# Two selective scans on one core: states written to the product ring in SBUF and multiplied there in place, PSUM left with the decays alone

## The chip, the cores and the metric

The kernel runs on one core of a Trainium2 chip, as one launch. The metric is the device time in microseconds (us) of that core; the time before is 5297.91 us, the median of three runs.

## What is computed

A residual network of four layers on an input of 32 x 256 tokens with 128 features. Each layer is `x = x + s * silu(f)`, where `s` comes from a recurrent or attention block and `f` from a feed-forward block. The change touches only the selective scan, which is the recurrent block of layer 3 and a part of that of layer 2 (layers are counted from 0). Cut to what matters:

```python
# layer 2, for each token t, 256 channels, 16 states per channel
dA = exp(dt[..., None] * A)
h  = h * dA + dt[..., None] * B[:, None, :] * x[..., None]
y  = sum(h * C[:, None, :], -1)
# layer 3
A_bar = exp(dt[..., None] * A)
B_bar = (A_bar - 1.0) / safe_A * B[:, None, :]
h = A_bar * h + B_bar * x[..., None]
y = einsum('bds,bs->bd', h, C) + D * x
```

The state starts at zero at the first token of each of the 32 sequences.

## The kernel before

`mamba` (L1411) is called twice, with `l3` false for layer 2 and true for layer 3. Both work on 16 tiles of 512 tokens (2 sequences of 256). A tile has 16 **units** (256 per layer): one half `h` of the 256 channels, which fills the 128 partitions, and two of the 16 states, so a unit's arrays are 128 x 1024 values of float32. The engines run their own loops over the units `q` and are tied by semaphores alone; the order on each engine is the order in which the code is written. For a unit:

- ACT, `decay(q)` (L1642): two exponentials write the decays into the PSUM array `ps_h` (in the trace `mb_h`), which has two buffers. Decay q overwrites what unit q-2 left there, so it waits for the reader of that: the scan, when POOL multiplies the unit, or else DVE's product.
- POOL, `u` (L1743): `u = B * (dt x)` into a ring of four (`m_u`), from the broadcast rows `m_bsb` that SP fetches by DMA. The input of unit q waits until scan q-4 is done.
- DVE, `make(q)`: in layer 3 a `scalar_tensor_tensor` (L1772) turns `u` into `(decay - 1) * u`; in both layers a memset (L1775) then puts zeros at the 4 places of `ps_h` where a sequence begins, so that one scan can run over both sequences and both states.
- DVE, `scan(q)` (L1786): `tensor_tensor_scan`, from the decays in PSUM and `u` in SBUF. It writes into `ps_h` in place, or, for the units that POOL multiplies (`by_pool`: every fourth in layer 2, every second in layer 3), into one of two SBUF buffers `m_hs`.
- the product with C, `times_c(q)`: on DVE (L1795) from `ps_h` in PSUM and the rows `m_csb` in SBUF, on POOL (L1722) from `m_hs` and `m_csb`. Both write the ring `hc` of four units in SBUF (`m_hc`; in layer 3 it lies in the large array that the trace calls `r`).
- PE, `sum_states(q)` (L1506): matmuls that add the unit's two products into `ps_y`. They run strictly in the order of q.

DVE's loop is, for each q:

```python
scan(q)
if q + 1 < NU:
    make(q + 1)
if not by_pool[q]:
    times_c(q)
```

and POOL's is `u(q)`, then `times_c(q - 3)` if that unit is its own. Once per tile come other steps: on POOL `step_sizes` (two sums into `m_dt`, L1707, and in layer 2 the product `m_dtx`, L1713) and in layer 3 `gate_old` (L1727, L1730); on DVE `gated` (L1804), `finish` (L1811, L1813) and in layer 3 `fix` (L1766).

Another stage is read for one fact only: `attention_inputs`, in which DVE (L1913, L1924, L1931) and POOL (L1968, L1973) work beside each other on 128 x 512 arrays.

Of the kernel before, what the change touches and what calls it, by code (L numbers as in the profile page):

```python
# [7 lines left out]
ALU = mybir.AluOpType  # L8
ACT = mybir.ActivationFunctionType
# [1401 lines left out]
def mamba(nc, w, parts, l3, hp, res, out, bc_d, gate_of=None):  # L1411

    wconv, a_neg, diag_y, diag_d, conv_bias, corr = parts
    with ExitStack() as ctx:
        def sb(name, shape, dt=F32):
            return ctx.enter_context(nc.sbuf_tensor(("m3_" if l3 else "m2_") + name, shape, dt))
# [12 lines left out]
        bsb = sb("bsb", [P, RING, SG, TILE])  # L1429
        csb = sb("csb", [P, RING, SG, TILE])  # L1430
        u = sb("u", [P, RING, SG, TILE])
        hc = out[:, 6 * TILE:(6 + RING * SG) * TILE].rearrange("p (n s t) -> p n s t", n=RING, s=SG) if l3 \
            else sb("hc", [P, RING, SG, TILE])
        hs = sb("hs", [P, 2, SG, TILE])
        yg = sb("yg", [P, 2, TILE])
        warm = sb("warm", [P, 3 * NT + 2])
        names = " ".join(f"b_in{s}" for s in range(RING)) + " " + " ".join(f"c_in{s}" for s in range(RING))
# [24 lines left out]
        @block.tensor  # L1462
        def _(pe):

            def conv(a, h):
                if a:
                    pe.wait_ge(sg_ready, 2 * a)
                for k in range(TAPS):
                    mm = nc.tensor.matmul(ps_w[:, h], wconv[:, k, h * P:(h + 1) * P], padded_tile(hp, k)(a),  # L1469
                                          start=k == 0, stop=k == TAPS - 1)  # L1470
                mm.then_inc(xs_in, 1)

            def gate(a, h):
                pe.wait_ge(dt_taken, 2 * a + 1 + h)
                if h == out_bank and a >= 2:
                    pe.wait_ge(x_done, a - 1)
                nc.tensor.matmul(ps_w[:, h], w["in_w"][:, DI + h * P:DI + (h + 1) * P], padded_tile(hp)(a),
                                 start=True, stop=True).then_inc(gate_in, 1)

            def project_bc(a):  # L1480
                pe.wait_ge(xs_ready, 2 * a + 2)
                for h in range(2):
                    mm = nc.tensor.matmul(ps_w[:, 0], w["xp_bc"][:, h * P:(h + 1) * P], xs[:, a % 2, h], start=h == 0, stop=h == 1)
                mm.then_inc(bc_in, 1)

            def project_low(a):
                for h in range(2):
                    mm = nc.tensor.matmul(ps_w[0:64, 1], w["xp_low"][:, h * 64:(h + 1) * 64], xs[:, a % 2, h],
                                          start=h == 0, stop=h == 1)
                mm.then_inc(low_in, 1)  # L1490

            def step_size(a, h):
                K = 64 if l3 else NSTATE
                pe.wait_ge(low_ready, a + 1)
                nc.tensor.matmul(ps_w[:, h], w["dt_w"][0:K, h * P:(h + 1) * P], low[0:K],
                                 start=True, stop=True).then_inc(dt_in, 1)

            def sum_states(q):
                i, g, h = place(q)
                if by_pool[q]:  # L1500
                    pe.wait_ge(hp_ready, pool_units[q + 1])
                else:
                    pe.wait_ge(hc_ready, dve_units[q + 1])
                for s in range(SG):
                    weight = diag_y[:, h * NSTATE + g * SG + s] if l3 else w["eye"]
                    mm = nc.tensor.matmul(ps_y[:, h], weight, hc[:, q % RING, s], start=False, stop=g == GROUPS - 1 and s == SG - 1)  # L1506
                mm.then_inc(y_used, 1)

            def project_out(i):
                pe.wait_ge(yg_ready, 2 * i + 2)  # L1510
                pe.wait_ge(dt_taken, 2 * min(i + 2, NT))
                if i == NT - 1:
                    pe.wait_ge(sg_ready, 2 * NT)
                    pe.wait_ge(x_done, i)
                for h in range(2):
                    mm = nc.tensor.matmul(ps_w[:, out_bank], w["out_w"][:, h * P:(h + 1) * P], yg[:, h],
                                          start=h == 0, stop=h == 1)
                mm.then_inc(out_ready, 1)

            def project(a):  # L1520
                project_bc(a)
                if l3:
                    project_low(a)

            conv(0, 0)
            conv(0, 1)
            project(0)
            step_size(0, 0)
            step_size(0, 1)
            gate(0, 0)  # L1530
            gate(0, 1)
            for i in range(NT):
                more = i + 1 < NT
                if more:
                    conv(i + 1, 0)
                    conv(i + 1, 1)
                if i:
                    pe.wait_ge(yg_ready, 2 * i)
                for h in range(2):
                    nc.tensor.matmul(ps_y[:, h], diag_d[:, h], xs[:, i % 2, h], start=True, stop=False)  # L1540
                for n in range(UNITS):
                    sum_states(i * UNITS + n)
                    if n == (3 if l3 else 2) and more:
                        project(i + 1)
                    if n == (5 if l3 else 3) and more:
                        step_size(i + 1, 0)
                        step_size(i + 1, 1)
                    if n == (9 if l3 else 7) and i:
                        project_out(i - 1)
                    if n == (11 if l3 else 10) and more:  # L1550
                        gate(i + 1, 0)
                        gate(i + 1, 1)
            project_out(NT - 1)

        @block.scalar
        def _(act):
# [75 lines left out]
            def decay(q):  # L1632

                i, g, h = place(q)
                act.wait_ge(dt_ready, 2 * i + h + 1)
                if q >= 2 and by_pool[q - 2]:
                    act.wait_ge(h_ready, q - 1)
                if q >= 2 and not by_pool[q - 2]:
                    act.wait_ge(hc_ready, dve_units[q - 1])
                for s in range(SG):  # L1640
                    n = h * NSTATE + g * SG + s
                    ins = nc.scalar.activation(ps_h[:, q % 2, s], dt[:, i % 2, h], ACT.Exp, scale=a_neg[:, n:n + 1])  # L1642
                ins.then_inc(da_ready, 1)

            for n in range(UNITS):
# [54 lines left out]
        def _(pool):  # L1700
# [13 lines left out]
                    pool.wait_ge(dtx_ready, a + 1)  # L1714

            def times_c(q):
                n, k = q // 2, pool_units[q]
                pool.wait_ge(h_ready, q + 1)
                pool.wait_ge(c_in[n % RING], (n // RING + 1) * 16)
                if q >= RING:  # L1720
                    pool.wait_ge(y_used, q - RING + 1)
                nc.gpsimd.tensor_tensor(hc[:, q % RING], hs[:, k % 2], csb[:, n % RING], ALU.mult).then_inc(hp_ready, 1)  # L1722

            def gate_old(a):
                pool.wait_ge(x_done, a + 1)
# [30 lines left out]
        def _(dve):  # L1756
            V = nc.vector

            def flat(ap):
                return ap.rearrange("p s t -> p (s t)")  # L1760
# [6 lines left out]

            def make(q):
                dve.wait_ge(da_ready, q + 1)
                if l3:  # L1770
                    dve.wait_ge(u_ready, q + 1)  # L1771
                    V.scalar_tensor_tensor(out=flat(u[:, q % RING]), in0=flat(ps_h[:, q % 2]), scalar=-1.0,  # L1772
                                           in1=flat(u[:, q % RING]), op0=ALU.add, op1=ALU.mult).then_inc(made, 1)
                    dve.wait_ge(made, q + 1)
                V.memset(ps_h[:, q % 2].rearrange("p s (r t) -> p (s r) t", t=T)[:, :, 0:1], 0.0).then_inc(cleared, 1)  # L1775

            def scan(q):
                if not l3:
                    dve.wait_ge(u_ready, q + 1)
                dve.wait_ge(cleared, q + 1)  # L1780
                to = ps_h[:, q % 2]
                if by_pool[q]:
                    to = hs[:, pool_units[q] % 2]
                    if pool_units[q] >= 2:
                        dve.wait_ge(hp_ready, pool_units[q] - 1)
                V.tensor_tensor_scan(flat(to), flat(ps_h[:, q % 2]), flat(u[:, q % RING]), 0.0,  # L1786
                                     ALU.mult, ALU.add).then_inc(h_ready, 1)

            def times_c(q):
                n = q // 2  # L1790
                dve.wait_ge(h_ready, q + 1)
                dve.wait_ge(c_in[n % RING], (n // RING + 1) * 16)
                if q >= RING:
                    dve.wait_ge(y_used, q - RING + 1)  # L1794
                V.tensor_tensor(hc[:, q % RING], ps_h[:, q % 2], csb[:, n % RING], ALU.mult).then_inc(hc_ready, 1)  # L1795

            def gated(i):

# [16 lines left out]
            if l3:  # L1815
                fix(0, 0)
                fix(0, 1)
            make(0)
            for q in range(NU):
                i, n = q // UNITS, q % UNITS  # L1820
                scan(q)
                if q + 1 < NU:
                    make(q + 1)
                if not by_pool[q]:
                    times_c(q)
# [1571 lines left out]
```

## Time and profile before

| | us |
|---|---|
| median of three runs (5293.03 to 5308.22) | 5297.91 |
| the profiled execution, its own time | 5317.53 |
| its span | 5315.9 |
| scan stage of layer 2, window 2065 to 2950 | 885 |
| scan stage of layer 3, window 4210 to 5310 | 1100 |

Times in the trace are counted from the start of the span. A row of grouped instructions gives their number, their busy time, the mean of one in ns, and the time that the engine sat idle before them with what ended it. In a timeline a start can lie a few hundredths of a microsecond before the end of the instruction ahead, since the engines overlap the end of one with the beginning of the next.

### The profile page before, as it was taken

Reading aid. Unit: us, or ns where it says so; the run is one execution under the profiler, and the core shown is the slowest. Engines: PE = TensorE matmul, PEld = TensorE weight load, DVE = VectorE, ACT = ScalarE, POOL = GpSimd, SP = SyncE. Lnnn points to the kernel's source line nnn. Section 1 sums busy time; section 2 is a strip of 40 time slices with the busy share of each in tenths; the row PEclk is TensorE's granted clock in tenths of the full one; section 3 lists DMA queues with packets and bytes.
Section 4 is the critical chain, followed back from the end, with each engine's and each line's share of the span. In section 5 each row is a group of like instructions: output and inputs, shape, how many; then the busy total and the mean of one; then the engine's idle time right before and its main releaser. Section 6 shows DMA issues by size and latency. Waiting matters only on the chain. (4 is left out here: it accounts for less than half of the span.)

```text
span 5315.9 us, 46819 instructions
## 1 busy us (share of the span) xinstructions
PE 3899.6 (73%) x13216; PEld 1770.4 (33%) x13216; DVE 3623.8 (68%) x5296; ACT 2530.9 (48%) x3893; POOL 2938.8 (55%) x2250
## 2 busy tenths in 40 slices
PE   5444425895583997888887879998698877777776
PEld 2111202472231564333333345454243322222222
DVE  6999615312253775999999744444444499999999
ACT  4444311232152776666665334445236555555554
POOL 3887470105404445999999311112431288988987
PEclk7777756897786998999999988889798899999999
DMA  1110210121121113444444232331110243444442
GB/s 47 40 42 8 82 47 5 46 67 47 44 92 42 52 50 114 154 156 156 152 155 152 65 65 40 41 41 31 40 52 9 83 135 137 134 139 135 136 140 99
DMA packets 161696, 434.74 MB, mean 82 GB/s; under 512 B 28150, under 2 KB 51384, under 8 KB 160048
## 3 DMA queue, kind: packets, MB, share of 16 engines
q1 hardware_dynamic: 142512, 374.41, 23.0%
q0 software_dynamic: 18944, 57.57, 3.0%
q8 instruction: 97, 1.59, 0.1%
q14 instruction: 143, 1.17, 0.1%
HBM read 363.67 MB, written 68.68 MB: 81 GB/s over the span
## 5 line engine op out<-in xcount | busy, mean ns | idle before, releaser
L1642 ACT ACTIVATE mb_h<-m_dt,m_a_neg 128x512 f32<-128x512 f32 x1024 | 665.7, 682 | 720.3 <-DVE r L1795 330.6
L1506 PE MATMUL mb_y<-r,m_diag_y 128*128 128x512 f32 x1024 | 547.2, 669 | 271.1 <-POOL r L1722 158.8
L1786 DVE TENSOR_TENSOR_SCAN mb_h<-mb_h,m_u 128x1024 f32<-128x1024 f32 x320 | 733.9, 2293 | 10.4
L1743 POOL TENSOR_TENSOR m_u<-m_bsb,m_dtx 128x1024 f32<-128x1024 f32 x256 | 596.2, 2357 | 20.8 <-DVE mb_h L1786 13.6
L1506 PE MATMUL mb_y<-m_hc,w_common 128*128 128x512 f32 x1024 | 494.2, 622 | 147.7 <-DVE m_hc L1795 84.7
L1743 POOL TENSOR_TENSOR m_u<-m_bsb,m_xs 128x1024 f32<-128x1024 f32 x256 | 599.6, 2367 | 0.0
L1786 DVE TENSOR_TENSOR_SCAN m_hs<-mb_h,m_u 128x1024 f32<-128x1024 f32 x192 | 437.6, 2279 | 0.2 <-POOL m_u L1743 0.2
L2259 DVE TENSOR_REDUCE at_mx<-at_ps_s 128x4 f32<-128x512 f32 (+1 forms) x256 | 243.2, 958 | 235.4 <-PE at_ps_s L2073 235.2
L1506 PEld LDWEIGHTS mb_y<-r,m_diag_y 128*128 128x128 f32 x1024 | 195.7, 207 | 617.1 <-POOL r L1722 238.7
L1722 POOL TENSOR_TENSOR r<-m_hs,m_csb 128x1024 f32<-128x1024 f32 x128 | 304.9, 2382 | 120.4 <-DVE m_hs L1786 119.3
L1506 PEld LDWEIGHTS mb_y<-m_hc,w_common 128*128 128x128 f32 x1024 | 190.0, 195 | 443.9 <-issue 192.2
L1772 DVE SCALAR_TENSOR_TENSOR m_u<-mb_h,m_u 128x1024 f32<-128x1024 f32 x256 | 308.0, 1203 | 19.2 <-ACT mb_h L1642 19.2
L2191 ACT ACTIVATE at_pt<-at_ps_c 128x512 f32<-128x512 f32 x384 | 229.1, 607 | 173.1 <-PE at_ps_c L2101 122.1
L2217 POOL CAST at_nm<-at_mx 128x16 bf16<-128x16 f32 x64 | 12.7, 198 | 521.1 <-DVE at_mx L2259 521.1
L343 PE MATMUL d_ring<-r,w_l 128*128 128x512 f32 x128 | 91.6, 859 | 224.1 <-ACT d_fm L393 222.2
L1469 PE MATMUL mb_w<-r,m_wconv 128*128 128x512 f32 x512 | 234.4, 611 | 22.3 <-ACT m_sg L1570 11.5
L1795 DVE TENSOR_TENSOR m_hc<-mb_h,m_csb 128x1024 f32<-128x1024 f32 x192 | 235.1, 1225 | 3.5
L493 POOL TENSOR_TENSOR d_sq_q<-d_state,d_tm 128x512 f32<-128x512 f32 x128 | 161.9, 1270 | 91.2 <-DVE d_state L597 91.0
L2098 PE MATMUL at_ps_c<-at_q,at_k 75*128 75x512 bf16 x384 | 157.7, 411 | 46.5 <-ACT at_pt L2191 26.9
L1707 POOL TENSOR_TENSOR m_dt<-m_lin,m_sp 128x512 f32<-128x512 f32 x64 | 80.0, 1274 | 202.2 <-ACT m_sp L1598 202.2
L2073 PE MATMUL at_ps_s<-at_k,at_q 72*128 72x256 bf16 (+1 forms) x1024 | 176.3, 267 | 0.0
L1004 POOL DMA_INDIRECT x_slots<-r,l_slots x128 | 124.8, 975 | 86.1 <-DVEq L1047 44.6
(503 smaller groups left out, 8714.4 us busy)
## 6 DMA issues: line engine op xcount, KB each, us to landing
m_bsb<-bc_rows SPq DMA_DIRECT2D x256, 512.0 KB, 4.8
m_csb<-bc_rows SPq DMA_DIRECT2D x256, 512.0 KB, 3.9
at_q<-q_parts SPq DMA_DIRECT2D x144, 128.0 KB
x_slots<-d_zeros SPq DMA_DIRECT2D x8, 1024.0 KB, 5.1
kept_x<-r SPq DMA_DIRECT2D x2, 4096.0 KB
xg_xg<-x_slots SPq DMA_DIRECT2D x32, 256.0 KB
y_slots<-xg_yo POOLq DMA_DIRECT2D x32, 256.0 KB
xl_xg<-x_slots SPq DMA_DIRECT2D x32, 256.0 KB
```

What stands on the lines that cost most here:

```text
L493: G.tensor_tensor(sq_q[:, 2 * p:2 * p + 2], state[:, n % 3], qt.unsqueeze(2).broadcast_to([P, 2 * HL, D0, D0]), ALU.mult).then_inc(sq_read ...
L1469: mm = nc.tensor.matmul(ps_w[:, h], wconv[:, k, h * P:(h + 1) * P], padded_tile(hp, k)(a), start=k == 0, stop=k == TAPS - 1)
L1506: mm = nc.tensor.matmul(ps_y[:, h], weight, hc[:, q % RING, s], start=False, stop=g == GROUPS - 1 and s == SG - 1)
L1642: ins = nc.scalar.activation(ps_h[:, q % 2, s], dt[:, i % 2, h], ACT.Exp, scale=a_neg[:, n:n + 1])
L1722: nc.gpsimd.tensor_tensor(hc[:, q % RING], hs[:, k % 2], csb[:, n % RING], ALU.mult).then_inc(hp_ready, 1)
L1743: nc.gpsimd.tensor_tensor(u[:, q % RING], bsb[:, n % RING], dtx[:, i % 2, h].unsqueeze(1).broadcast_to([P, SG, TILE]), ALU.mult).then_inc( ...
L1772: V.scalar_tensor_tensor(out=flat(u[:, q % RING]), in0=flat(ps_h[:, q % 2]), scalar=-1.0, in1=flat(u[:, q % RING]), op0=ALU.add, op1=ALU.m ...
L1786: V.tensor_tensor_scan(flat(to), flat(ps_h[:, q % 2]), flat(u[:, q % RING]), 0.0, ALU.mult, ALU.add).then_inc(h_ready, 1)
L1795: V.tensor_tensor(hc[:, q % RING], ps_h[:, q % 2], csb[:, n % RING], ALU.mult).then_inc(hc_ready, 1)
L2073: mm = nc.tensor.matmul(ps_s[:, g % 2, d, 0:keys], q9[0:PARTS, slot, g * QPK + d, col:col + P], k9[0:PARTS, slot, g, row:row + keys], star ...
L2191: nc.scalar.activation(pt[:, u % 8], ps_c[:, u % 2], ACT.Exp).then_inc(exp_ready, 1)
L2259: V.tensor_reduce(mx[:, n % 2, g * QPK:(g + 1) * QPK], ps_s[:, g % 2, :, 0:(n % 2 + 1) * P], AX, ALU.max, negate=True).then_inc(max_ready, 1)
```

## The change

- Every scan now writes to the ring `hc` in SBUF, none to PSUM, and `hs` is gone. The ring has six units in layer 2 and five in layer 3 (`held`), and it is the scan, no longer the product, that waits until PE has summed the unit whose place it takes.
- The product with C is made in place in the ring, by DVE or POOL as before.
- PSUM holds decays alone. A decay waits only for the scan two units back, never for a product. In layer 2 the zeros are written once, at the start, and ACT leaves their columns out (`rows(to)[:, :, 1:T]`); `make` is gone from the loop there. In layer 3 `make` stays as it was.
- `project_out(i)` waits for the step sizes of tile i+2 instead of i+1.

```diff
-        hc = out[:, 6 * TILE:(6 + RING * SG) * TILE].rearrange("p (n s t) -> p n s t", n=RING, s=SG) if l3 \
-            else sb("hc", [P, RING, SG, TILE])
-        hs = sb("hs", [P, 2, SG, TILE])
+        held = 5 if l3 else 6
+        hc = out[:, 6 * TILE:(6 + held * SG) * TILE].rearrange("p (n s t) -> p n s t", n=held, s=SG) if l3 \
+            else sb("hc", [P, held, SG, TILE])
...
-                pe.wait_ge(dt_taken, 2 * min(i + 2, NT))
+                pe.wait_ge(dt_taken, 2 * min(i + 3, NT))
...
-                if q >= 2 and by_pool[q - 2]:
+                if q >= 2:
                     act.wait_ge(h_ready, q - 1)
-                if q >= 2 and not by_pool[q - 2]:
-                    act.wait_ge(hc_ready, dve_units[q - 1])
+                elif not l3:
+                    act.wait_ge(cleared, 1)
...
-                    ins = nc.scalar.activation(ps_h[:, q % 2, s], dt[:, i % 2, h], ACT.Exp, scale=a_neg[:, n:n + 1])
+                    to, step = ps_h[:, q % 2, s], dt[:, i % 2, h]
+                    if not l3:
+                        to, step = rows(to)[:, :, 1:T], rows(step)[:, :, 1:T]
+                    ins = nc.scalar.activation(to, step, ACT.Exp, scale=a_neg[:, n:n + 1])
...
-                if q >= RING:
-                    pool.wait_ge(y_used, q - RING + 1)
-                nc.gpsimd.tensor_tensor(hc[:, q % RING], hs[:, k % 2], csb[:, n % RING], ALU.mult).then_inc(hp_ready, 1)
+                nc.gpsimd.tensor_tensor(hc[:, q % held], hc[:, q % held], csb[:, n % RING], ALU.mult).then_inc(hp_ready, 1)
...
             def scan(q):
-                if not l3:
-                    dve.wait_ge(u_ready, q + 1)
-                dve.wait_ge(cleared, q + 1)
-                to = ps_h[:, q % 2]
-                if by_pool[q]:
-                    to = hs[:, pool_units[q] % 2]
-                    if pool_units[q] >= 2:
-                        dve.wait_ge(hp_ready, pool_units[q] - 1)
-                V.tensor_tensor_scan(flat(to), flat(ps_h[:, q % 2]), flat(u[:, q % RING]), 0.0,
+                if l3:
+                    dve.wait_ge(cleared, q + 1)
+                else:
+                    dve.wait_ge(da_ready, q + 1)
+                    dve.wait_ge(u_ready, q + 1)
+                if q >= held:
+                    dve.wait_ge(y_used, q - held + 1)
+                V.tensor_tensor_scan(flat(hc[:, q % held]), flat(ps_h[:, q % 2]), flat(u[:, q % RING]), 0.0,
                                      ALU.mult, ALU.add).then_inc(h_ready, 1)
 
             def times_c(q):
                 n = q // 2
                 dve.wait_ge(h_ready, q + 1)
                 dve.wait_ge(c_in[n % RING], (n // RING + 1) * 16)
-                if q >= RING:
-                    dve.wait_ge(y_used, q - RING + 1)
-                V.tensor_tensor(hc[:, q % RING], ps_h[:, q % 2], csb[:, n % RING], ALU.mult).then_inc(hc_ready, 1)
+                V.tensor_tensor(hc[:, q % held], hc[:, q % held], csb[:, n % RING], ALU.mult).then_inc(hc_ready, 1)
...
-            make(0)
+                make(0)
+            else:
+                V.memset(ps_h.rearrange("p n s (r t) -> p (n s r) t", t=T)[:, :, 0:1], 0.0).then_inc(cleared, 1)
             for q in range(NU):
                 i, n = q // UNITS, q % UNITS
                 scan(q)
-                if q + 1 < NU:
+                if l3 and q + 1 < NU:
                     make(q + 1)
```

How the instructions stand on DVE, in the listing of the program (where the scan is printed as SCALAR_TENSOR_TENSOR). Before, layer 2, around a unit that POOL multiplies:

```order
 L1786 SCALAR_TENSOR_TENSOR mb_h<-mb_h,m_u 128x1024
 L1775 MEMSET mb_h 128x4
 L1795 TENSOR_TENSOR m_hc<-mb_h,m_csb 128x1024
 L1786 SCALAR_TENSOR_TENSOR m_hs<-mb_h,m_u 128x1024
 L1775 MEMSET mb_h 128x4
 L1786 SCALAR_TENSOR_TENSOR mb_h<-mb_h,m_u 128x1024
 L1775 MEMSET mb_h 128x4
 L1795 TENSOR_TENSOR m_hc<-mb_h,m_csb 128x1024
```

and the same place in the changed program:

```order
 L1785 SCALAR_TENSOR_TENSOR m_hc<-mb_h,m_u 128x1024
 L1792 TENSOR_TENSOR m_hc<-m_hc,m_csb 128x1024
 L1785 SCALAR_TENSOR_TENSOR m_hc<-mb_h,m_u 128x1024 x2
 L1792 TENSOR_TENSOR m_hc<-m_hc,m_csb 128x1024
 L1785 SCALAR_TENSOR_TENSOR m_hc<-mb_h,m_u 128x1024
```

The memsets are gone, two scans stand next to each other where POOL multiplies the first, and the product (now L1792) reads two arrays in SBUF where it read PSUM and SBUF. In layer 3, before, a pair of units (the first POOL's, the second DVE's):

```order
 L1786 SCALAR_TENSOR_TENSOR m_hs<-mb_h,m_u 128x1024
 L1772 SCALAR_TENSOR_TENSOR m_u<-mb_h,m_u 128x1024
 L1775 MEMSET mb_h 128x4
 L1786 SCALAR_TENSOR_TENSOR mb_h<-mb_h,m_u 128x1024
 L1772 SCALAR_TENSOR_TENSOR m_u<-mb_h,m_u 128x1024
 L1775 MEMSET mb_h 128x4
 L1795 TENSOR_TENSOR r<-mb_h,m_csb 128x1024
```

and changed:

```order
 L1785 SCALAR_TENSOR_TENSOR r<-mb_h,m_u 128x1024
 L1772 SCALAR_TENSOR_TENSOR m_u<-mb_h,m_u 128x1024
 L1775 MEMSET mb_h 128x4
 L1785 SCALAR_TENSOR_TENSOR r<-mb_h,m_u 128x1024
 L1772 SCALAR_TENSOR_TENSOR m_u<-mb_h,m_u 128x1024
 L1775 MEMSET mb_h 128x4
 L1792 TENSOR_TENSOR r<-r,m_csb 128x1024
```

The order is the same; only the places that the scans write and the product reads differ. POOL's order is unchanged in both layers.

## Rows read from the trace of the kernel before

**Rows 1.** The two scan stages as windows: length, then each engine's busy us
```profile
2065.00:2950.00 885.00, 728.61 (x1572) 293.31 (x1572) 842.45 (x752) 566.22 (x846) 816.40 (x366) 0.98 0.45 151
4210.00:5310.00 1100.00, 814.60 (x1632) 306.13 (x1632) 1064.62 (x974) 600.50 (x888) 972.02 (x446) 0.94 0.39 133
```
**Rows 2.** Waits in layer 2: us in total, times, longest
```profile
DVE mb_h L1775 <- ACT mb_h L1642: 55.1, 32, 33.1
```
**Rows 3.** Line 1795: layer 2's products on DVE, min/median/max ns, first and last start
```profile
L1795 DVE TENSOR_TENSOR m_hc<-mb_h,m_csb x192: 1224/1225/1226, 2073.6 to 2942.1; 128x1024 f32<-128x1024 f32 x192
```
**Rows 4.** POOL's groups of instructions in the window of layer 2
```profile
L1743 POOL TENSOR_TENSOR m_u<-m_bsb,m_dtx 128x1024 f32<-128x1024 f32 x256 | 596.2, 2357 | 20.8 <-DVE mb_h L1786 13.6 <-PE mb_y L1506 5.8
L1722 POOL TENSOR_TENSOR m_hc<-m_hs,m_csb 128x1024 f32<-128x1024 f32 x64 | 150.6, 2352 | 31.7 <-DVE m_hs L1786 31.7
L1713 POOL TENSOR_TENSOR m_dtx<-m_dt,m_xs 128x1024 f32<-128x1024 f32 x16 | 37.6, 2349 | 1.3
L1707 POOL TENSOR_TENSOR m_dt<-m_lin,m_sp 128x512 f32<-128x512 f32 x30 | 37.4, 1270 | 0.0
```
**Rows 5.** POOL's products in the window of layer 3
```profile
L1722 POOL TENSOR_TENSOR r<-m_hs,m_csb 128x1024 f32<-128x1024 f32 x128 | 304.9, 2382 | 120.4 <-DVE m_hs L1786 119.3
```
**Rows 6.** DVE's timeline in layer 2 (start us, duration us)
```profile
2571.77 2.29 DVE L1786 TENSOR_TENSOR_SCAN mb_h<-mb_h,m_u 128x1024 f32<-128x1024 f32 x1
...
2574.09 1.22 DVE L1795 TENSOR_TENSOR m_hc<-mb_h,m_csb 128x1024 f32<-128x1024 f32 x1
2575.23 2.28 DVE L1786 TENSOR_TENSOR_SCAN m_hs<-mb_h,m_u 128x1024 f32<-128x1024 f32 x1
...
2577.68 2.30 DVE L1786 TENSOR_TENSOR_SCAN mb_h<-mb_h,m_u 128x1024 f32<-128x1024 f32 x1
```
**Rows 7.** DVE's timeline at layer 2's last unit, where no memset follows the scan
```profile
2939.73 2.29 DVE L1786 TENSOR_TENSOR_SCAN mb_h<-mb_h,m_u 128x1024 f32<-128x1024 f32 x1
2942.05 1.22 DVE L1795 TENSOR_TENSOR m_hc<-mb_h,m_csb 128x1024 f32<-128x1024 f32 x1
```
**Rows 8.** DVE's groups in the stage that prepares attention, window 2990 to 3075
```profile
L1913 DVE TENSOR_TENSOR ai_prod<-ai_ps,w_attention 128x512 f32<-128x512 f32 x32 | 21.8, 689 | 9.1 <-PE ai_ps L1889 8.2
L1931 DVE TENSOR_TENSOR ai_prod<-ai_prod 128x512 f32<-128x512 f32 x16 | 18.0, 1125 | 0.3
...
L1924 DVE TENSOR_TENSOR ai_kprod<-ai_kprod 128x512 f32<-128x512 f32 x4 | 2.8, 692 | 0.1
```
**Rows 9.** DVE's timeline in that stage
```profile
3010.44 1.66 DVE L1931 TENSOR_TENSOR ai_prod<-ai_prod 128x512 f32<-128x512 f32 x1
...
3014.10 1.18 DVE L1931 TENSOR_TENSOR ai_prod<-ai_prod 128x512 f32<-128x512 f32 x1
```
**Rows 10.** POOL's timeline at the same place
```profile
3010.39 1.16 POOL L1968 TENSOR_TENSOR ai_prod<-ai_prod,ai_qs 128x512 f32<-128x512 f32 x1 [4.28 <-ACT ai_qs L1956]
...
3013.57 1.16 POOL L1968 TENSOR_TENSOR ai_prod<-ai_prod,ai_qs 128x512 f32<-128x512 f32 x1 [0.46 <-ACT ai_qs L1956]
3014.69 1.61 POOL L1973 TENSOR_TENSOR ai_qs<-ai_prod,ai_qs 128x512 bf16<-128x512 f32 x1
```
**Rows 11.** DVE's timeline in layer 3, one pair of units
```profile
4710.71 2.28 DVE L1786 TENSOR_TENSOR_SCAN m_hs<-mb_h,m_u 128x1024 f32<-128x1024 f32 x1
...
4714.27 2.30 DVE L1786 TENSOR_TENSOR_SCAN mb_h<-mb_h,m_u 128x1024 f32<-128x1024 f32 x1
...
4717.83 1.22 DVE L1795 TENSOR_TENSOR r<-mb_h,m_csb 128x1024 f32<-128x1024 f32 x1
4718.97 2.28 DVE L1786 TENSOR_TENSOR_SCAN m_hs<-mb_h,m_u 128x1024 f32<-128x1024 f32 x1
```
**Rows 12.** POOL's timeline in the same pair
```profile
4713.07 2.42 POOL L1722 TENSOR_TENSOR r<-m_hs,m_csb 128x1024 f32<-128x1024 f32 x1 [1.26 <-DVE m_hs L1786]
4715.39 4.71 POOL L1743 TENSOR_TENSOR m_u<-m_bsb,m_xs 128x1024 f32<-128x1024 f32 x2
4721.33 2.38 POOL L1722 TENSOR_TENSOR r<-m_hs,m_csb 128x1024 f32<-128x1024 f32 x1 [1.22 <-DVE m_hs L1786]
```

More of the change, by code:

```diff
@@ L1505, in sum_states @@
                     weight = diag_y[:, h * NSTATE + g * SG + s] if l3 else w["eye"]
-                    mm = nc.tensor.matmul(ps_y[:, h], weight, hc[:, q % RING, s], start=False, stop=g == GROUPS - 1 and s == SG - 1)
+                    mm = nc.tensor.matmul(ps_y[:, h], weight, hc[:, q % held, s], start=False, stop=g == GROUPS - 1 and s == SG - 1)
                 mm.then_inc(y_used, 1)
@@ L1716, in times_c @@
             def times_c(q):
-                n, k = q // 2, pool_units[q]
+                n = q // 2
                 pool.wait_ge(h_ready, q + 1)
                 pool.wait_ge(c_in[n % RING], (n // RING + 1) * 16)
-                if q >= RING:
-                    pool.wait_ge(y_used, q - RING + 1)
-                nc.gpsimd.tensor_tensor(hc[:, q % RING], hs[:, k % 2], csb[:, n % RING], ALU.mult).then_inc(hp_ready, 1)
+                nc.gpsimd.tensor_tensor(hc[:, q % held], hc[:, q % held], csb[:, n % RING], ALU.mult).then_inc(hp_ready, 1)
             def gate_old(a):
@@ L1769, in make @@
                 dve.wait_ge(da_ready, q + 1)
-                if l3:
-                    dve.wait_ge(u_ready, q + 1)
-                    V.scalar_tensor_tensor(out=flat(u[:, q % RING]), in0=flat(ps_h[:, q % 2]), scalar=-1.0,
-                                           in1=flat(u[:, q % RING]), op0=ALU.add, op1=ALU.mult).then_inc(made, 1)
-                    dve.wait_ge(made, q + 1)
+                dve.wait_ge(u_ready, q + 1)
+                V.scalar_tensor_tensor(out=flat(u[:, q % RING]), in0=flat(ps_h[:, q % 2]), scalar=-1.0,
+                                       in1=flat(u[:, q % RING]), op0=ALU.add, op1=ALU.mult).then_inc(made, 1)
+                dve.wait_ge(made, q + 1)
                 V.memset(ps_h[:, q % 2].rearrange("p s (r t) -> p (s r) t", t=T)[:, :, 0:1], 0.0).then_inc(cleared, 1)
             def scan(q):
-                if not l3:
+                if l3:
+                    dve.wait_ge(cleared, q + 1)
+                else:
+                    dve.wait_ge(da_ready, q + 1)
                     dve.wait_ge(u_ready, q + 1)
-                dve.wait_ge(cleared, q + 1)
-                to = ps_h[:, q % 2]
-                if by_pool[q]:
-                    to = hs[:, pool_units[q] % 2]
-                    if pool_units[q] >= 2:
-                        dve.wait_ge(hp_ready, pool_units[q] - 1)
-                V.tensor_tensor_scan(flat(to), flat(ps_h[:, q % 2]), flat(u[:, q % RING]), 0.0,
+                if q >= held:
+                    dve.wait_ge(y_used, q - held + 1)
+                V.tensor_tensor_scan(flat(hc[:, q % held]), flat(ps_h[:, q % 2]), flat(u[:, q % RING]), 0.0,
                                      ALU.mult, ALU.add).then_inc(h_ready, 1)
```

## The prediction, made before the changed kernel was run

> **What bounds the kernel now.** I read the two scan stages only, since the change touches nothing else. First the windows [rows 1]: in layer 2 DVE is busy 842 of 885 us and POOL 816; in layer 3 DVE 1065 of 1100 and POOL 972. PE has 729 and 815, ACT some 600. So DVE sets the pace and POOL is close behind. Then the timelines, for the cycle of DVE. In layer 2 a unit that DVE multiplies takes 3.46 us from scan to scan (2571.77 to 2575.23) and one that POOL multiplies 2.45 (2575.23 to 2577.68) [rows 6], so a group of four takes 3 x 3.46 + 2.45 = 12.83. The first and the last product of the layer, units 1 and 255, stand 868.5 us apart [rows 3]: 3.42 us a unit, 54.7 a tile. That is 4 x 12.83 plus 3.4. Of the 3.4, ACT's late decays are 55.1 - 33.1 = 22 us in the layer (the 33.1 is the wait at its start) [rows 2], 1.4 a tile; 2.0 are DVE's steps that come once per tile. In layer 3 a pair of units takes 8.26 us (4710.71 to 4718.97) [rows 11], 66.1 a tile without those steps.
>
> **POOL's load.** Its instructions follow each other every 2.32 to 2.33 us [rows 12]. A tile of layer 2 has 16 inputs and 4 products, 46.6 us, and 2 x 1.27 + 2.35 = 4.9 for the step sizes [rows 4]: 51.5 of 54.7. In layer 3, 24 x 2.33 = 55.9 and four sums of about 1.27, 5.1 together: 61.0. There POOL sits idle before its product 120 us in all, waiting for the scan [rows 5].
>
> **The change part by part.**
>
> *The memset leaves layer 2.* Its 62 ns hide almost wholly: with it the product starts 2.32 us after its scan's start [rows 6], without it, at the layer's last unit, also 2.32 [rows 7]. Only where two scans now stand together is there a gain: 2.45 becomes about 2.21 (a scan's 2.28 less the 0.07 by which independent instructions overlap), 0.24 us x 64 = 15 us. A group is then 12.59.
>
> *Decays wait for scans only.* At most the 22 us of ACT's lateness go. DVE of layer 2 alone would thus gain 37 us. If it did, POOL (816 busy of then 848) would just not be in the way.
>
> *Scans write SBUF.* 2.28 for 2.30 [rows 11]; 3 us in layer 3. The new wait of the scan for PE's sum of five or six units back is free: PE has 156 and 285 us to spare in the stages [rows 1], and the sum of a POOL unit follows its product by one unit, with two more in the ring. The later wait of `project_out` is met before PE gets there, as ACT has taken those step sizes a unit before. The columns that ACT leaves out are 4 of 1024.
>
> *The product reads two arrays in SBUF.* This is the part that I think decides, and the scan stages before never show it: scan, `make` and product each had one operand in PSUM. The stage that prepares attention shows it. A 128 x 512 product takes DVE 689 ns with an operand in PSUM and 692 with both in SBUF where POOL is idle, but the sum at L1931, also both in SBUF, has a mean of 1125 [rows 8]. The timelines say why: at 3010.44 it took 1.66, and POOL had started 0.05 earlier and ended at 3011.55; at 3014.10 it took 1.18, and POOL's instruction ended at 3014.73 [rows 9, 10]. Taking 0.69 for the work, it began at 3011.41 and 3014.59, both 0.14 before POOL's end. POOL is held in turn: its next one, at 3014.69, took 1.61 instead of 1.16, so it began at 3015.14, 0.14 before DVE's end at 3015.28 [rows 9, 10]. So one waits until the other is through, they alternate, and whoever starts first, even by 0.05, has the way. The product of 1.225 us [rows 3] thus bars POOL for 1.085, and an instruction of POOL of 2.36 bars the product for 2.22.
>
> The Trainium skill ("SBUF — State Buffer", "Who interferes with whom") says that a DVE instruction with two SBUF inputs and a GpSimd instruction that reads SBUF exclude each other for the whole instruction; the trace agrees except for the 0.14. Without it the forecast would be some 36 us higher (0.14 x 256 waits). The skill also gives DVE a fixed part of 58 cycles with SBUF sources and 120 with PSUM ("VectorE: DVE Perf Modes", "The TRN2 errata"); by it 320 products would save 0.065 us each, 21 us, and the sum be 5683. The rows speak against it: 692 against 689 ns, no gain.
>
> *Layer 2 with the exclusion.* Floor first: 51.5 of POOL plus 12 products of 1.085 = 64.5 us a tile against 54.7, +157 us for 16 tiles. Now by hand, from a product starting at 0. POOL starts at 1.085 and, if it has work, again at 3.415. DVE's scan starts at 1.14 and its product is ready at 1.14 + 2.32 = 3.46. POOL is ahead by 0.04 and the product waits to 3.415 + 2.22 = 5.63: 2.15 us. After a POOL unit (two scans) the product is ready at 5.66 and POOL would start its next at 5.745, so it goes at once. With a backlog a group takes 12.59 + 2 x 2.15 = 16.9 and POOL does 6 instructions in it. If POOL has none, its u(q+4) waits for scan q. It starts 0.08 after the scan's end (4710.71 + 2.28 to 4713.07) [rows 11, 12], the product 0.03 after it [rows 7], so the product wins; such a group has one wait, 14.8 us, and 5 instructions. A tile needs 20 and 4.9 us, as much as 22: two groups of each kind, 63.4, and DVE's 2.0. That is **65.4 a tile, +171 us**. Bounds: the floor, +157, and all groups at 16.9, 69.6 a tile, +238.
>
> *Layer 3 with the exclusion.* From the end of the scan that POOL waits for, at 4712.99, POOL's product starts at +0.08, its first input at +2.40, its second at 4715.39 + 4.71 - 2.37 = 4717.73, +4.74 [rows 12]. DVE's product starts at 4717.83, +4.84 [rows 11], and in the changed kernel 0.02 earlier. POOL is first by 0.08, and the product waits until 4717.73 + 2.37 - 0.14 = 4719.96: **2.1 us in a pair**. The pattern keeps itself up, for POOL then idles until the next scan ends and starts from it again. All 128 pairs make +270. Once per tile POOL's 5.1 us put it out of step; a lengthened pair leaves it 10.4 - 7.0 - 1.1 = 2.3 spare, so for some 2.5 pairs the wait is anything up to 2.1, and I take 1.2. A tile: 5.5 x 2.1 + 2.5 x 1.2 = 14.6, **+235 us** in the layer. Bounds +200 and +270.
>
> **Sum.** +171 + 235 = +406. On the profiled execution, 5317.5 + 406 = 5724; on the median, which lies 19.6 below it, **5704 us**. This case's own range is 5655 to 5806 (+357 to +508).
>
> **Rivals.**
>
> *Layer 3 falls in step.* The 0.08 there are thin. If DVE's product gets in before POOL's second input, POOL does it during the next scan and nothing waits; the layer then costs only POOL's sum, 61.0 + 8 x 1.085 = 69.7 a tile against DVE's 66.1 and some 2.0 for its steps once per tile, +26 us. With layer 2 at its floor to forecast, +183 to +197: 5481 to 5495. For it: the margin. Against it: the 0.05 that sufficed at 3010.44. 18%.
>
> *POOL wins in layer 2 too.* If the semaphore of the scan served POOL's input before DVE's product, each of the 12 products waits 2.15: 12.59 + 6.45 = 19.0 a group, 78 a tile, +375, and with layer 3 at +270, 5943 us. Against it: 0.08 and 0.03 above. 9%.
>
> *Faster.* The other side: the products find the way free. The gain is then the 22 of ACT, 15 between scans and 3 in layer 3, 40 us: 5258 us. It decides from 40 / 320 = 0.125 us a product: if the mean product takes less than 1.35 us, the kernel is faster. For it: none of the waits seen was of a 128 x 1024 instruction in these stages. Against it: POOL is busy for over nine tenths of layer 2, and each instruction of DVE that met it in rows 9 was held. 8%.
>
> *The change moves only what was hidden.* Waits near 0.125 us, and the sum comes to nothing within 0.3% (16 us, about what a measurement of this kernel can tell from no change). 4%.
>
> PE is no rival: layer 2's tile has 729 / 16 = 45.5 us of it at a granted clock of 0.98 [rows 1], and the tile grows to 65.
>
> **How the numbers follow.** The forecast has 61%, and its time is the prediction. 5460 to 5820 adds the first rival, 79% together. Slower by over 0.3%: 61 + 18 + 9 = 88%; within: 4%; faster: 8%.
>
> **What would show it.** DVE's product (L1792) should have a minimum near 1225 ns, a maximum near 3.4 us, and a mean of about 2.4 us in layer 2 (mean wait (171 + 37) / 192 = 1.1) and 3.1 in layer 3 (235 / 128 = 1.8 more); POOL's inputs should lengthen to as much as 3.4 us; scans and memsets should keep 2.28 and 0.062. DVE's cycle in layer 3 should read 10.4 us a pair. A product near 1225 ns throughout proves me wrong at the root; one at 2.4 in layer 2 but 1.3 in layer 3 is the first rival; layer 2 near 78 a tile the second.

## The result, and the profile after

The changed kernel takes 5621.65 us (5612.45 to 5627.06, four runs) against 5303.07 us for the kernel before in the same comparison: a ratio of 1.0602, 95% interval 1.0582 to 1.0623, or +318.6 us. Forecast were +406, with a range of +162 to +522; the sum's own bounds were +357 to +508. The profiled execution has a span of 5610.8 us. One of the twelve executions of e8_psum_products, below, took 9989 us, and its ratio is formed without it.

First the windows of the two scan stages (length, busy us of PE, its weight loads, DVE, ACT and POOL, then PE's granted clock, the DMA share and GB/s), which answer to [rows 1]:

```profile
2058.00:3085.00 1027.00, 788.90 (x1572) 310.36 (x1572) 974.82 (x495) 567.29 (x849) 1002.99 (x368) 0.92 0.39 131
4325.00:5605.00 1280.00, 911.11 (x1634) 334.11 (x1632) 1242.31 (x974) 596.30 (x889) 1027.51 (x446) 0.85 0.35 115
```

Though DVE has 257 instructions fewer in layer 2, it is busy for 132 us more, and POOL, whose instructions are the same, for 187 us more. PE's clock is lower too (0.85 for 0.94 in layer 3), but PE is not what DVE waits for: DVE's waits for it come to 2.2 us in layer 2 and 5.3 in layer 3. Lines 1792 (DVE's product) and 1744 (POOL's inputs) say where (min/median/max in ns, first and last start), beside [rows 3]:

```profile
L1792 DVE TENSOR_TENSOR m_hc<-m_hc,m_csb x192: 1224/1296/3374, 2069.3 to 3078.3; 128x1024 f32<-128x1024 f32 x192
L1792 DVE TENSOR_TENSOR r<-r,m_csb x128: 1224/3310/3342, 4342.5 to 5596.4; 128x1024 f32<-128x1024 f32 x128
```
```profile
L1744 POOL TENSOR_TENSOR m_u<-m_bsb,m_dtx x256: 2332/3319/3387, 2062.2 to 3065.8; 128x1024 f32<-128x1024 f32 x128
L1744 POOL TENSOR_TENSOR m_u<-m_bsb,m_xs x256: 2331/2353/3406, 4329.2 to 5578.3; 128x1024 f32<-128x1024 f32 x128
```

Both are stretched: a product takes up to 3.37 us instead of 1.225, an input up to 3.41 instead of 2.4. The wait thus shows as busy time, inside the instruction that is held, and not as idle time. DVE's groups, with the busy time and the mean of a product, 1987 ns in layer 2 and 2642 in layer 3:

```profile
L1792 DVE TENSOR_TENSOR m_hc<-m_hc,m_csb 128x1024 f32<-128x1024 f32 x192 | 381.6, 1987 | 6.6
L1792 DVE TENSOR_TENSOR r<-r,m_csb 128x1024 f32<-128x1024 f32 x128 | 338.2, 2642 | 0.0
```

All 320 products follow one rule. At the start of 225 of them POOL is inside an instruction that has 0.2 us or more left, and each of these is stretched; less 1.225 us for the work, they begin 0.14 us before POOL's end (0.137 to 0.147). The other 95 take 1227 ns at most. From the first to the last product, layer 2 takes 1009.0 us (868.5 before) and layer 3 1253.9 (1076.5 before, from 4226.0 to 5302.5): +140.5 and +177.4, together 318.

The cycle in layer 3 is the one worked out. DVE's timeline and POOL's, one pair of units, beside [rows 11, 12]:

```profile
4847.80 3.33 DVE L1792 TENSOR_TENSOR r<-r,m_csb 128x1024 f32<-128x1024 f32 x1
4851.06 2.27 DVE L1785 TENSOR_TENSOR_SCAN r<-mb_h,m_u 128x1024 f32<-128x1024 f32 x1
...
4858.14 3.32 DVE L1792 TENSOR_TENSOR r<-r,m_csb 128x1024 f32<-128x1024 f32 x1
```
```profile
4843.08 2.35 POOL L1723 TENSOR_TENSOR r<-r,m_csb 128x1024 f32<-128x1024 f32 x1 [3.36 <-DVE r L1785]
4845.39 4.67 POOL L1744 TENSOR_TENSOR m_u<-m_bsb,m_xs 128x1024 f32<-128x1024 f32 x2
4853.41 2.35 POOL L1723 TENSOR_TENSOR r<-r,m_csb 128x1024 f32<-128x1024 f32 x1 [3.36 <-DVE r L1785]
```

POOL's second input starts at 4845.39 + 4.67 - 2.36 = 4847.70, DVE's product 0.10 later, and it waits 2.1 us. POOL then stands idle for 3.36 us until the next scan ends, and starts the same race again. A pair takes 4858.14 - 4847.80 = 10.34 us.

In layer 2 a group of four units that begins with POOL's reads, on DVE:

```profile
2592.26 4.46 DVE L1785 TENSOR_TENSOR_SCAN m_hc<-mb_h,m_u 128x1024 f32<-128x1024 f32 x2
2596.75 1.29 DVE L1792 TENSOR_TENSOR m_hc<-m_hc,m_csb 128x1024 f32<-128x1024 f32 x1
2597.97 2.28 DVE L1785 TENSOR_TENSOR_SCAN m_hc<-mb_h,m_u 128x1024 f32<-128x1024 f32 x1
2600.28 3.37 DVE L1792 TENSOR_TENSOR m_hc<-m_hc,m_csb 128x1024 f32<-128x1024 f32 x1
2603.57 2.28 DVE L1785 TENSOR_TENSOR_SCAN m_hc<-mb_h,m_u 128x1024 f32<-128x1024 f32 x1
2605.88 1.23 DVE L1792 TENSOR_TENSOR m_hc<-m_hc,m_csb 128x1024 f32<-128x1024 f32 x1
2607.03 4.46 DVE L1785 TENSOR_TENSOR_SCAN m_hc<-mb_h,m_u 128x1024 f32<-128x1024 f32 x2
```

One product of three waits in full, and the group takes 2607.03 - 2592.26 = 14.77 us: the 14.8 that the prediction gave a group with one wait.

### The profile page after: what moved, and what is told of

Same layout as the page of the kernel before. It is cut to its first block and busy times, and to the rows that moved or that the text cites. A ratio compares the mean times of both kernels' runs of the same rounds, so it can differ in the third digit from the quotient of the medians.

```text
span 5610.8 us, 46691 instructions
## 1 busy us (share of the span) xinstructions
PE 4034.9 (72%) x13216; PEld 1805.9 (32%) x13216; DVE 3934.3 (70%) x5041; ACT 2522.6 (45%) x3893; POOL 3176.3 (57%) x2250
## 5 line engine op out<-in xcount | busy, mean ns | idle before, releaser
L1645 ACT ACTIVATE mb_h<-m_dt,m_a_neg 128x510 f32<-128x510 f32 (+1 forms) x1024 | 661.4, 679 | 1039.7 <-DVE r L1785 625.0
L1506 PE MATMUL mb_y<-r,m_diag_y 128*128 128x512 f32 x1024 | 620.2, 744 | 349.4 <-DVE r L1792 223.2
L1744 POOL TENSOR_TENSOR m_u<-m_bsb,m_dtx 128x1024 f32<-128x1024 f32 x256 | 735.5, 2897 | 5.7
L1506 PE MATMUL mb_y<-m_hc,w_common 128*128 128x512 f32 x1024 | 533.8, 663 | 187.6 <-DVE m_hc L1792 132.7
L1744 POOL TENSOR_TENSOR m_u<-m_bsb,m_xs 128x1024 f32<-128x1024 f32 x256 | 642.8, 2530 | 0.0
L1785 DVE TENSOR_TENSOR_SCAN m_hc<-mb_h,m_u 128x1024 f32<-128x1024 f32 x256 | 578.7, 2276 | 61.8 <-POOL m_u L1744 61.5
L1785 DVE TENSOR_TENSOR_SCAN r<-mb_h,m_u 128x1024 f32<-128x1024 f32 x256 | 584.5, 2283 | 4.5 <-DVE mb_h L1775 0.7
L1723 POOL TENSOR_TENSOR r<-r,m_csb 128x1024 f32<-128x1024 f32 x128 | 301.2, 2353 | 243.4 <-DVE r L1785 242.2
L1792 DVE TENSOR_TENSOR m_hc<-m_hc,m_csb 128x1024 f32<-128x1024 f32 x192 | 381.6, 1987 | 6.6
L1792 DVE TENSOR_TENSOR r<-r,m_csb 128x1024 f32<-128x1024 f32 x128 | 338.2, 2642 | 0.0
L1710 POOL TENSOR_TENSOR m_dt<-m_lin,m_sp 128x512 f32<-128x512 f32 x64 | 94.5, 1496 | 202.2 <-ACT m_sp L1598 202.2
```

The lines of the kernel that those rows point to most:

```text
L1506: mm = nc.tensor.matmul(ps_y[:, h], weight, hc[:, q % held, s], start=False, stop=g == GROUPS - 1 and s == SG - 1)
L1645: ins = nc.scalar.activation(to, step, ACT.Exp, scale=a_neg[:, n:n + 1])
L1723: nc.gpsimd.tensor_tensor(hc[:, q % held], hc[:, q % held], csb[:, n % RING], ALU.mult).then_inc(hp_ready, 1)
L1744: nc.gpsimd.tensor_tensor(u[:, q % RING], bsb[:, n % RING], dtx[:, i % 2, h].unsqueeze(1).broadcast_to([P, SG, TILE]), ALU.mult).then_inc( ...
L1785: V.tensor_tensor_scan(flat(hc[:, q % held]), flat(ps_h[:, q % 2]), flat(u[:, q % RING]), 0.0, ALU.mult, ALU.add).then_inc(h_ready, 1)
L1792: V.tensor_tensor(hc[:, q % held], hc[:, q % held], csb[:, n % RING], ALU.mult).then_inc(hc_ready, 1)
```

## The experiments

**Theories.** A: a DVE product with both inputs in SBUF and a POOL instruction that reads SBUF exclude each other, and who starts first goes first. B: the cost lies in the scans' new places or waits. C: the two contend, but order does not decide. These runs were made on three chips that do the kernel before in 4988.6, 4993.2 and 4995.9 us (medians), so a time is compared with that of the kernel before on its own chip, and runs from different chips by their ratios to it. The scan stages last as long there as in the first comparison (1009.0 and 1253.9 us in e12); 260 us of the difference lie before layer 2's scan, and were not looked into.

**e1_psum_operand.** Scans, ring and the scans' waits are as changed; the product's operand moves back to PSUM, and with it the wait of ACT's decay for that product.

```diff
                 if q >= 2:
                     act.wait_ge(h_ready, q - 1)
+                    if not by_pool[q - 2]:
+                        act.wait_ge(hc_ready, dve_units[q - 1])
...
-V.tensor_tensor(hc[:, q % held], hc[:, q % held], csb[:, n % RING], ALU.mult)
+V.tensor_tensor(hc[:, q % held], ps_h[:, q % 2], csb[:, n % RING], ALU.mult)
```

> The changed kernel, but DVE's product takes its first operand from PSUM (the decays of its unit, so it multiplies the wrong array: the product of state and C is left out), and a decay waits for the product again, as before the change; scans still write the ring in SBUF, their wait for PE's sums and the missing memsets of layer 2 stay. Theory A (two SBUF inputs exclude POOL): every product takes 1225 ns, POOL's inputs 2.36 us at most 2.4, the time falls to 5255 to 5305 us. Theory B (the cost lies in the scans' new wait for PE or in writing SBUF, and the long products are a symptom): the time stays over 5550 us.

4951.8 us, ratio 0.992 (0.9898 to 0.9941). DVE's groups:

```profile
L1794 DVE TENSOR_TENSOR m_hc<-mb_h,m_csb 128x1024 f32<-128x1024 f32 x192 | 235.0, 1224 | 6.6
L1794 DVE TENSOR_TENSOR r<-mb_h,m_csb 128x1024 f32<-128x1024 f32 x128 | 156.6, 1224 | 0.0
```

One operand's place takes away the whole loss and leaves a gain of 44 us, 41 of it in layer 2 (827.3 us from first to last product). B falls. The 44 are what the rest of the change is worth; the prediction had 40. They include the end of ACT's lateness, though the decays wait for the product again here: past its first wait DVE waited 22 us for them in layer 2 of the kernel before, and waits 0.3 us in e1.

**e2_layer2_only** and **e3_layer3_only** have the change in one layer and call the `mamba` of before for the other.

> The change in layer 2 only, layer 3 as before. Both theories take the layers as separate: 5303 + 140 = 5443 us (5430 to 5455), by the 868.5 us of before and the 1009.0 us after between the first and the last product of layer 2. A sum of the two layers' costs that differs from 318 us by over 20 would mean that they interact.

> The change in layer 3 only, layer 2 as before: 5303 + 177 = 5480 us (5465 to 5495), by 1076.5 us before and 1253.9 us after between the first and last product of layer 3.

5136.9 and 5175.9 against 4995.9 us: +141 and +180. The layers' costs add up (321), and each is what its own stage showed.

**e4_nudge.**

```diff
+                if l3 and q % 2 == 1:
+                    nc.gpsimd.memset(nudge[:, q:q + 1], 0.0)
                 nc.gpsimd.tensor_tensor(u[:, q % RING], bsb[:, n % RING], ...
```

> The changed kernel with one tiny memset (128 x 1, about 0.1 us, into a buffer that nothing reads) on POOL ahead of its input of every odd unit of layer 3, which makes POOL start its third instruction of a pair about 0.1 us later. Theory A with first come, first served: POOL's lead of 0.08 us is lost, DVE's product goes first at 1225 ns in most pairs, the pair falls from 10.3 to 8.3 us and layer 3 by about 150 us, so the kernel takes 5460 to 5490 us though POOL has more to do. Rival C (POOL always has the way, or an average contention without regard to order): no gain, 5620 us or some more, up to 5650.

5324.1 us, ratio 1.0659 (1.0640 to 1.0679), no gain. By the time alone this is what C expected; POOL's timeline and DVE's tell why it decided nothing:

```profile
4625.94 0.11 POOL L1746 MEMSET m_nudge<- 128x1 f32 x1
4625.99 2.35 POOL L1747 TENSOR_TENSOR m_u<-m_bsb,m_xs 128x1024 f32<-128x1024 f32 x1
```
```profile
4626.05 3.37 DVE L1795 TENSOR_TENSOR r<-r,m_csb 128x1024 f32<-128x1024 f32 x1
```

The memset overlaps its neighbours, moves the input by 0.05 us, and POOL is still 0.06 ahead.

**e5_nudge_more** adds `pool.wait_ge(u_ready, q)` ahead of the memset.

> As e4_nudge, whose memset moved POOL's third instruction of a pair by only 0.03 to 0.05 us and left it 0.05 ahead; now POOL also waits for its own input before (a semaphore wait) ahead of the memset, which should move it by 0.1 to 0.2 us, behind DVE's product. Theory A with first come, first served: products of layer 3 mostly 1225 ns, a pair 8.3 us, from the first to the last product of layer 3 about 1105 us instead of 1254, so 5165 to 5185 us against 4996 for the kernel before on this chip (ratio 1.034 to 1.038). Rival C (order of arrival does not decide): 5325 us or more, the products still at 3.3 us.

5161.4 us, ratio 1.0345 (1.0317 to 1.0372). POOL's timeline and DVE's:

```profile
4622.10 0.10 POOL L1747 MEMSET m_nudge<- 128x1 f32 x1
4622.16 3.28 POOL L1748 TENSOR_TENSOR m_u<-m_bsb,m_xs 128x1024 f32<-128x1024 f32 x1
```
```profile
4622.01 1.23 DVE L1796 TENSOR_TENSOR r<-r,m_csb 128x1024 f32<-128x1024 f32 x1
```

Now DVE is ahead by 0.15. Its product takes 1.23, and POOL's input, 3.28, bears the wait during the next scan, where it costs nothing. Layer 3 takes 1115.8 us from first to last product (1105 expected, 1253.9 without):

```profile
L1796 DVE TENSOR_TENSOR r<-r,m_csb x128: 1224/1226/3479, 4029.7 to 5145.5; 128x1024 f32<-128x1024 f32 x128
```

91 of the 128 products do not wait, where 31 did not in the changed kernel. Against the kernel before on its chip the loss is 173 us, where the changed one loses 316 (e12): an added wait and an added instruction take some 140 us off and make the kernel 2.7% faster than the changed one (1.0345 against 1.0626). C falls.

**e6_pool_writes_only.** The code, cut:

```diff
-nc.gpsimd.tensor_tensor(u[:, q % RING], bsb[:, n % RING], dtx..., ALU.mult).then_inc(u_ready, 1)
+if q:
+    pool.wait_ge(u_ready, q)
+nc.gpsimd.memset(fill[:], 0.5)
+nc.gpsimd.memset(u[:, q % RING], 0.5).then_inc(u_ready, 1)
```

> The changed kernel, but POOL's inputs are left out (the product of B and dt x): in their place POOL fills a buffer of 1700 columns and then the 1024 of the input with a constant, about 2.3 us together, so it is as busy but only writes SBUF. POOL's products with C still read. If the exclusion is of SBUF reads, DVE's product takes 1225 ns whenever it meets a fill, and only those that meet a product or a step size of POOL are longer: mean under 1.5 us in layer 2 and layer 3. If any use of SBUF by POOL excludes DVE, the means stay at 2.0 and 2.6 us or above, with maxima by the length of a fill.

4996.9 us in a single execution, so its time is read roughly and its trace is what counts. DVE's groups, then a product on DVE beside POOL's fills:

```profile
L1795 DVE TENSOR_TENSOR m_hc<-m_hc,m_csb 128x1024 f32<-128x1024 f32 x192 | 271.6, 1415 | 6.6
L1795 DVE TENSOR_TENSOR r<-r,m_csb 128x1024 f32<-128x1024 f32 x128 | 160.1, 1251 | 0.0
...
4609.65 1.23 DVE L1795 TENSOR_TENSOR r<-r,m_csb 128x1024 f32<-128x1024 f32 x1
```
```profile
4608.67 0.94 POOL L1748 MEMSET m_u<- 128x1024 f32 x1
4609.76 1.51 POOL L1747 MEMSET m_fill<- 128x1700 f32 x1
```

The fill starts inside the product and neither is stretched; over all 512 fills the range is 1504 to 1535 ns. The other order is there too: 167 of the 320 products start while a fill or the memset of an input is running, and none of them takes over 1227 ns. POOL is about as busy as in the kernel before (975 of 1090 us in layer 3's window, against 972 of 1100 [rows 1]), yet the only waits left are those on its products and step sizes, which still read, and layer 3 takes 1076.1 us from first to last product, for 1076.5 before. DVE's product still reads two arrays in SBUF and writes in place here, so neither costs anything by itself. It is POOL's reading that excludes.

**e7_product_first** swaps `make(q + 1)` and `times_c(q)` in layer 3.

> The changed kernel, with DVE's product of layer 3 placed right behind its scan, ahead of make of the next unit. Theory A: it now asks at 3.60 us after the scan that POOL waits for, inside POOL's second instruction (2.40 to 4.72), and waits until 4.62, so 1.0 us instead of 2.1: products about 2.2 us where POOL is in step, a pair 9.4 us, layer 3 some 1200 to 1215 us from the first to the last product instead of 1254, the kernel 40 to 55 us faster than the changed one. Rival C (a mean contention whatever the order): no difference within 10 us.

5304.2 us, ratio 1.0638 (1.0615 to 1.0661), not told apart from the changed kernel's 1.0626: the gain of 40 to 55 us did not come, and by its time the run came out as rival C had it. The pair did come out as worked out. The products of two pairs in step:

```profile
4608.67 2.21 DVE L1792 TENSOR_TENSOR r<-r,m_csb 128x1024 f32<-128x1024 f32 x1
...
4618.08 2.20 DVE L1792 TENSOR_TENSOR r<-r,m_csb 128x1024 f32<-128x1024 f32 x1
```

They start 9.41 us apart, and 80 of the 128 products wait 0.98 us, where C has no reason for a change. But the mean product is 2402 ns, 0.24 less than 2642 and not 1.0: the 48 others now wait 1.5 us on average, for 0.3 in the changed kernel. And I forgot a term. A product right behind its own scan starts 2.32 us after it, where `make` started after 2.20, and without its wait the pair takes 9.41 - 0.98 = 8.43 us, 0.2 more than the 8.23 of a pair without a wait in the changed kernel. 128 x (0.24 - 0.2) = 5 us is what the stage shows (1248.7 us for 1253.9); this sum was made after the result.

**e9_dve_products** makes `by_pool` empty in layer 2.

> The changed kernel with all products of layer 2 on DVE (by_pool empty there); layer 3 as changed. The sum of what needs SBUF's shared read side then falls from 20 x 2.33 + 4.9 + 12 x 0.97 = 63.1 us a tile (measured 63.6) to 16 x 2.33 + 4.9 + 16 x 0.97 = 57.7, and DVE alone takes 16 x 3.46 + 2.0 = 57.4. Theory A with the sum as the floor: layer 2 from first to last product falls from 1009 to between 925 and 990 us (some waits of a whole POOL instruction stay), 20 to 85 us off the kernel, though DVE has 64 products more. Rival: DVE's own waits set the time, each of 256 products waits 0.76 us on average: 16 x (57.4 + 12.2) = 1110 us, slower by 100 us.

5280.1 us, 29 less than the changed kernel on the same chip (e12), with 64 products moved onto DVE. Layer 2 takes 978.4 us for units 0 to 255, 61.4 a tile, inside what was expected. The sum of the times of both engines' reads orders the two versions rightly. The mean product takes 1496 ns, 0.27 us of it waiting; 16 of them add 4.3 us to DVE's own 57.4 and give 61.7. So it is DVE with its waits that sets the time, as the rival had it, with a third of the rival's wait.

**e12_change_again** is the changed kernel on one of these chips, that of e9, e10 and e11.

> The changed kernel once more, on the chip of these experiments: ratio 1.060 to 1.066 against the kernel before (319 us on 4996), layer 3's first to last product 1254 us, so that e4, e7 and e9 can be held against it.

5309.5 us, ratio 1.0626 (1.0599 to 1.0653); layer 3 1253.9 us.

**Versions that beat both.** e8_psum_products keeps DVE's units in PSUM and lets POOL multiply its own in place in the ring; it also moves two of DVE's products a tile of layer 2 ahead of the next memset (`late`). e10 and e11 give POOL more of layer 3 besides. The code of e11 against the kernel before, cut:

```diff
-        by_pool = [q % (2 if l3 else 4) == 0 for q in range(NU)]
+        by_pool = [q % (2 if l3 else 4) == 0 or (l3 and q % UNITS in (7, 13)) for q in range(NU)]
...
-                nc.gpsimd.tensor_tensor(hc[:, q % RING], hs[:, k % 2], csb[:, n % RING], ALU.mult).then_inc(hp_ready, 1)
+                nc.gpsimd.tensor_tensor(hc[:, q % RING], hc[:, q % RING], csb[:, n % RING], ALU.mult).then_inc(hp_ready, 1)
...
+                late = not l3 and n in (5, 14)
+                if late:
+                    times_c(q)
```

> The kernel before with the part of the change that does not make DVE read two SBUF arrays: units that POOL multiplies are scanned into the ring and multiplied there in place (no m_hs), DVE's units stay in PSUM; in layer 2 DVE's product of the 6th and 15th unit of a tile goes ahead of the next memset, where DVE waited 0.6 to 0.8 us for ACT's decay. Theory A: no product over 1226 ns, and 32 times 0.55 us gained, 10 to 20 us faster than the kernel before (ratio 0.996 to 0.998). If the ring itself costs (its wait for PE's sums on DVE), it comes out slower.

> As e8_psum_products, with unit 7 of every tile of layer 3 multiplied by POOL too, nine of 16. No DVE instruction has two SBUF inputs, so POOL can take more at no cost to DVE: POOL 61.0 + 2.3 = 63.3 us a tile, DVE 68 - 1.1 = 67. 18 us faster than e8, so ratio 0.993 to 0.996 against the kernel before.

> As e10_nine_on_pool with unit 13 as well, ten of 16: POOL 65.7 us a tile, DVE 65.8. Up to 36 us faster than e8 if both fit, ratio 0.990 to 0.995; POOL becomes the bound and it comes out no better than e10 if the order of its instructions leaves gaps.

Ratios 0.9982 (0.9969 to 0.9995), 0.9944 (0.9925 to 0.9964) and 0.9933 (0.9915 to 0.9950). e8 gains 0.2%, at the edge of what can be told from nothing and just short of the 0.2 to 0.4% expected: layer 2 takes 861.6 us for 868.5 from first to last product, layer 3, where only the place of POOL's units differs, 1076.3 for 1076.5. With ten units of 16 on POOL layer 3 takes 1045.9 us from first to last product (1076.5 before), and DVE's products stay at 1224 ns; e10 and e11 are not told apart. e11, 4958.7 us against 4993.2 for the kernel before, has the lowest median of the versions that leave nothing out.

## Why the prediction held, and where its size was off

- **The step that decides** held: two inputs in SBUF, exclusion, the first one first. e1 shows the operand as the cause, e6 POOL's reading, e5 the order.
- **The size** was too high, 406 us for 318.6. The time lies in the stated range of 5460 to 5820 only because that was stretched downward for the first rival, which did not occur; that much is luck. The forecast's own range, 5655 to 5806, misses 5621.65 by 33 us, and each layer came out under its lower bound (+140.5 under +157, +177.4 under +200). The mean products were too high with it: 1.99 us in layer 2 and 2.64 in layer 3, for 2.4 and 3.1. (The forecast's own mean wait of 1.1 us gives 2.3 for layer 2, not 2.4; and its 0.14 x 256 should be 0.14 x 224, since it counts 6 waits a tile in layer 2 and 8 in layer 3.)
- **The memset, the decays and the scans' place**: 40 us of gain expected, 44 in e1. The sum is right, but its term of 22 us stands under the wrong cause: the decays' freedom from the product is not needed for it, as e1 has the gain without it. What gives it is the memset, which before asked for the next decay ahead of the product: in e8, which keeps the memsets and puts the product ahead of them in two units a tile, DVE's waits for ACT in layer 2 fall from 22 to 7 us past the first.
- **Layer 3**, +235 against +177.4. The pair in step is right, 10.34 for 10.4, and 80 of the 128 products wait over 1.95 us; I had 5.5 a tile, 88, which is 19 us of the miss. Mis-sized above all was the rest, 33 us: I took 1.2 us for each of 2.5 pairs a tile. There are three, and they wait 0.3 on average: 31 products not at all, 17 for 0.9. Out of step, DVE mostly comes first. The waits come to 181 us; less the 4 that the scans' new place gave (the prediction had 3 and did not put them into its sum) they are the 177.
- **Layer 2**, +171 against +140.5. The group's 14.77 is right, but only one group in four has two full waits, where I had two in four: 50 products wait in full and 30 for 1.2 us on average, with 48 short ones of 0.07 some 147 us, where two groups of each kind would give 208. In exchange a wait came that I had not listed, scans for POOL's input; the total, the number and the longest, then such a wait on DVE, and POOL's step sizes just before it:

```profile
DVE m_hc L1785 <- POOL m_u L1744: 61.5, 16, 27.1
...
2633.28 1.22 DVE L1792 TENSOR_TENSOR m_hc<-m_hc,m_csb 128x1024 f32<-128x1024 f32 x1
2636.80 4.60 DVE L1785 TENSOR_TENSOR_SCAN m_hc<-mb_h,m_u 128x1024 f32<-128x1024 f32 x2 [2.29 <-POOL m_u L1744]
```
```profile
2626.46 3.48 POOL L1710 TENSOR_TENSOR m_dt<-m_lin,m_sp 128x512 f32<-128x512 f32 x2
```

Less the 27.1 at the start of the stage these are 34 us, 2.3 once a tile, behind POOL's step sizes: while POOL makes them no inputs come, DVE runs out of them, and its products meet fewer of POOL's instructions. In e1 the same waits come to 27.1 us with 26.3 at the start, so they are new. 147 + 34 less the gains of 41 gives 140. The floor of 64.5 us a tile was too high too (measured 63.6): each change from POOL to DVE saves the 0.11 between 2.33 and 2.22, which I had worked out and not subtracted, 1.3 us a tile.
- **The rivals.** Layer 3 in step did not occur, but e5 made it in most pairs: +173 us on its chip, where the rival had +183 to +197, though layer 3 alone cost 39 us and not 26. That POOL wins every race of layer 2 too, and the faster case, did not occur.

## What to carry to other kernels

Moving an operand from PSUM to SBUF can cost more than every instruction it saves: count which DVE instructions then have two inputs in SBUF while POOL reads there, and take the sum of both engines' times, less their overlap, as a first floor (it put e9 and the changed kernel in the right order, and lay 0.4 to 3.7 us a tile too low). If such a pair can't be avoided, look in the timelines at who starts first: in layer 3 POOL's start fell from 0.10 us ahead to 0.15 behind, and that was worth some 140 us. Where DVE keeps one operand in PSUM, more work on POOL cost DVE's products nothing here (e10, e11: 1224 ns throughout).

## What was not expected of the hardware

- The race is sharp: with POOL's instruction 0.06 us ahead DVE's product waited 2.1 us (e4), with DVE's 0.15 ahead POOL's waited 0.9 (e5).
- Where the operand lies changes nothing while POOL is not in the way: the shortest product takes 1224 ns with both inputs in SBUF (changed kernel) and with one in PSUM (kernel before).
- A POOL instruction that only writes SBUF does not hold back a DVE instruction with two SBUF inputs, nor is it held (e6: 1.23 us and 1.51 us side by side).
- A memset of 128 x 1 on POOL takes 0.10 us by its row and moves the next instruction by 0.05 only (e4).
